# Two head layers' projections in three rounded terms, with the norm's scale and shift folded into weights and biases

## The chip, the cores and the metric

One core of a Trainium2 chip runs the kernel. The metric is the time of one execution on the device, in microseconds (us); a change of a few us in some 2060 is looked for.

## What is computed

The input is x, 16 batches of 256 tokens by 256 features, and a context of the same shape. Four layers follow one another, each added to x:

```python
x = x + L0_xattn(layernorm(x), ctx)          # cross attention, one head
x = x + L0_ffn(x)                            # norm, 32 heads of 8, wo, experts by place, gelu
x = x + L1_xattn(layernorm(x), ctx)          # cross attention with a self score
x = x + L1_ffn(x)                            # norm, 16 heads of 16, wo, norm, router, top 2 of 8 experts

# the part that the change is about, in both ffn layers:
xn = (x - mu) / sqrt(var + 1e-5) * ln_g + ln_b
q, k, v = xn @ wq + bq, xn @ wk + bk, xn @ wv + bv     # no bq, bk, bv in L0
```

All is fp32. The kernel before computes these six projections as fp32 matmuls, the scores of the heads from k and q that are each split into a rounded number and its rest (fp32r, the type in which PE multiplies at the faster rate).

## The kernel before

The batches go through six parts: A (first cross attention), B1 (norm and k, q, v of the 32 heads), B2 (wo, residual, FFN), C (second cross attention), D1 (norm and k, q, v of the 16 heads), D2 (wo, norm, router's logits); HB and HD are the heads themselves. Behind the last batch come the routing and a stage of experts, which has three rounded terms already (line 1837).

The parts of several batches run at once, in 19 rounds r = -1 to 17. Each engine has its own in-order program, cut into steps, and the steps belong to threads: S (scores, line 903, and their maxima, line 1270), T (turn of the maxima), E (exponentials, lines 940 and 1519), V (values, line 955), P (B2, C and D1 of batch r-1, the functions lin2), Q (A and B1 of batch r+1, D2 of batch r-2, the functions lin1), R (routing). A string of letters per round says in which order the threads take their next step, the same on all engines; twelve of the rounds (r = 2 to 13) use the string ORDER. In a round the heads of D1 of one batch and of B1 of the next have their scores; then the round's end holds B1 and D1 of the batches behind them.

At the end of such a round stand, in this order on PE: the turn of NP (line 847; NP is the normed x of D1), B1's key product, a turn of the maxima (MT, line 920), D1's key and query products, B1's query product, D1's and B1's value products, the turn of CXA (the next context), and then the first scores of the heads whose keys and queries D1 has just made. Names that end in Q belong to lin1, in P to lin2.

- `product` (line 854) makes a projection: four fp32 matmuls 128x128x256 (two output halves, two input halves), shown as 8 records.
- `take_cols` (line 1507) on ACT copies the turned norm out of PSUM with the norm's gain as scale and its shift as bias, one instruction for each half, into nTQ or nTP. `take` (line 1500) does so without scale, in one instruction of 128x512.
- The rounded head of the keys and queries is ACT's (line 1591, 1595 for B1, one instruction; line 1645 for D1, two with a bias), its rest is DVE's `rest` (line 1254 for B1, line 1252 for D1). Tiles are used again: qTQ, PRQ, pTQ, cTQ hold B1's keys, rests, queries, rests, and PRP, pTP, cTP, cxTP those of D1; nTQ is the tile of the turned norm.
- SP writes heads and rests to k_dram and q_dram (`put`, line 620, 16 issues in a round) and reads them back in the layout of the scores into KS and QS (`fetch`, line 626). The scores of D1's heads wait for that.
- `norm` on DVE (lines 1231 to 1244) needs POOL's power (line 748) in the middle.
- XF is the sum behind wo in B2 (it is in PRP); its turned copy XFT is in qTP. ACT copies it out of PSUM (line 1500) just ahead of the FFN's first product.

Of the kernel before, what the change touches and what calls it, by code (L numbers as in the profile page):

```python
# [20 lines left out]
F32 = mybir.dt.float32  # L21
# [6 lines left out]
P = 128  # L28
# [94 lines left out]

SECOND = "SPTSEQEQSPQEETEVVSSSQTSSTSPQSSEQPSQPSEEPTSPESQPVPESEVVPSPETPPPSPESQQPEPVSEVQSEQTSQEQQVSPPEQSPEPPVETQEVEQPPEVPPPEPQV"
# [7 lines left out]
def schedule(n, threads):  # L132

    def round_(r, par, b=True, p=True, a=True, d=True, order=ORDER):  # L140
        running = threads(r, par, b, p, a, d)
        for name in order:
            next(running[name])

    round_(-1, 1, b=False, p=False, d=False)
    round_(0, 0, p=False, d=False, order=SECOND)
    round_(1, 1, d=False, order=THIRD)
    for r in range(2, n - 2):
        round_(r, r % 2)
    round_(n - 2, 0, order=FOURTH)  # L150
    round_(n - 1, 1, a=False, order=EARLY)
    round_(n, 0, b=False, a=False, order=LATE)
    round_(n + 1, 1, b=False, p=False, a=False, order=LAST)
# [232 lines left out]
def layers(nc, a, out, scratch, sem, ident, ones, cst, logits, bank, routes):  # L386
# [13 lines left out]
    with ExitStack() as stack:  # L400
# [3 lines left out]
        def tile(name, dt=F32):  # L404
            return sb(name, [P, 2, D], dt)


        MA, WA, MC, WvC = tile("MA"), tile("WA"), tile("MC"), tile("WvC")
        wB = {n: tile(f"wB_{n}") for n in ("wq", "wk", "wv", "wo")}
        wD = {n: tile(f"wD_{n}") for n in ("wq", "wk", "wv", "wo")}  # L410
        wr = sb("wr", [P, DC, NE])
        cols, b1T = sb("cols", [P, 24]), sb("b1T", [P, B, FC])
# [6 lines left out]
        X0, CXA, XBA, NQ, nTQ, cxTQ, qTQ, PRQ, pTQ, cTQ = (  # L419
            tile(n) for n in ("X0", "CXA", "XBA", "NQ", "nTQ", "cxTQ", "qTQ", "PRQ", "pTQ", "cTQ"))  # L420
        X1, Y = [tile(f"X1{i}") for i in range(2)], [tile(f"Y{i}") for i in range(2)]
        zTQ, KHQ, KLQ, QHQ, QLQ = nTQ, qTQ, PRQ, pTQ, cTQ
# [4 lines left out]
        AOP, X2, XBP, NP, nTP, CXC, cxTP, qTP, PRP, pTP, cTP, YB = (  # L427
            tile(n) for n in ("AOP", "X2", "XBP", "NP", "nTP", "CXC", "cxTP", "qTP", "PRP", "pTP", "cTP", "YB"))
        X3 = [tile(f"X3{i}") for i in range(2)]
        AOTP, XF, XFT, prT, YD, zTP = nTP, PRP, qTP, pTP, X2, nTP  # L430
# [10 lines left out]
        HT = sb("HT", [P, FC, 2 * P])  # L441
# [56 lines left out]
        def col(name, c):  # L498
# [8 lines left out]
        s_spare, s_fill = sem("s_spare"), sem("s_fill")  # L507
        SPARES, FILLS = (8, 16), 4
# [12 lines left out]
               "B1": Events(sem("dve_B1"), "bn mv uw n kl ql"), "HB": Events(sem("dve_HB"), "rh0 os0 rh1 os1 rh2 os2 rh3 os3"),  # L521
               "B2": Events(sem("dve_B2"), "xf x"),
               "C": Events(sem("dve_C"), "bn mv uw n c0 c max mxs mxc nb z rs diag x"),
               "D1": Events(sem("dve_D1"), "bn mv uw n kl ql v"), "HD": Events(sem("dve_HD"), "rh0 os0 rh1 os1"),
# [312 lines left out]
        def _(t):  # L837
# [19 lines left out]

            t.transpose(bank[0][:, 0:NV], vecs, ident[0:NV, 0:NV])
# [101 lines left out]

            def threads(r, par, b_, p_, a_, d_):
                hd, hb = lined_up(r, b_, d_)
                last = hd[1] if hd else hb[1] if hb else None
                shared = {}
                if last:
                    h, b = last
                    shared = {"os": (h.os, now(t, b * h.groups + h.groups)), "shifted": (h.shifted, now(t, b * h.twos + h.twos))}
# [24 lines left out]
            def lin1(b, e, par, a_, d_):  # L992
# [8 lines left out]
                if a_:  # L1001
                    wait(t, act, "A", b, "cxT")
                    wait(t, dve, "A", b, "n")
                    turn(5, NQ).then_inc(*E.tick("nT"))
                yield
                if a_:
                    wait(t, act, "A", b, "nT")
                    product(5, MA, nTQ).then_inc(*E.tick("qT"))
                yield
                if a_:  # L1010
                    wait(t, act, "A", b, "qT")
                    product(5, qTQ, cxTQ).then_inc(*E.tick("s"))
                yield
                if a_:
                    wait(t, act, "A", b, "exp")
                    turn(5, PRQ).then_inc(*E.tick("pT"))
                yield
# [1013 lines left out]
```

## Time and profile before

| what | value |
|---|---|
| median of 3 runs | 2061.82 us (2059.59 to 2388.49) |
| profiled execution, its own time | 2058.43 us |
| its span in the trace | 2056.6 us |
| busy share of PE, DVE, ACT, POOL | 92%, 66%, 48%, 29% |
| mean granted clock of PE | 0.952 |

A row of the timeline gives the start, the length, the engine, the line, what is written from what, the shape and in brackets the idle time ahead of it with what ended it. "x8" means that eight records of a kind follow each other; the length then runs from the first one's start to the last one's end. A granted clock of 1.00 is 2.4 GHz, one of 0.50 is 1.2 GHz. The busy share of a whole span mixes stretches with different limits, so what a step is worth is read in its own stretch.

### The profile page before, as it was taken

Reading aid. Unit: us, or ns where it says so; the run is one execution under the profiler, and the core shown is the slowest. Engines: PE = TensorE matmul, PEld = TensorE weight load, DVE = VectorE, ACT = ScalarE, POOL = GpSimd, SP = SyncE. Lnnn points to the kernel's source line nnn. Section 1 sums busy time; section 2 is a strip of 40 time slices with the busy share of each in tenths; the row PEclk is TensorE's granted clock in tenths of the full one; section 3 lists DMA queues with packets and bytes.
Section 4 is the critical chain, followed back from the end, with each engine's and each line's share of the span. In section 5 each row is a group of like instructions: output and inputs, shape, how many; then the busy total and the mean of one; then the engine's idle time right before and its main releaser. Section 6 shows DMA issues by size and latency. Waiting matters only on the chain. (4 is left out here: it accounts for less than half of the span.)

```text
span 2056.6 us, 37550 instructions
## 1 busy us (share of the span) xinstructions
PE 1890.6 (92%) x13657; PEld 1445.2 (70%) x13657; DVE 1353.9 (66%) x3466; ACT 994.1 (48%) x1956; POOL 606.2 (29%) x490
## 2 busy tenths in 40 slices
PE   5699999999999999999999999999887659999998
PEld 4466767777766767677776777766666439999997
DVE  2456667676767767675766767676765457677664
ACT  1255556565556556555655656655343223333332
POOL 0102131221303121220313121230223046777674
PEclk8789999999999999999999999999989759999999
DMA  5223441515244351514344251414120254444231
GB/s 191 87 88 124 139 159 65 175 55 170 100 131 145 122 175 50 174 65 159 122 151 152 73 175 55 165 60 149 59 78 11 72 178 91 119 91 88 43 44 25
DMA packets 205704, 224.86 MB, mean 109 GB/s; under 512 B 15083, under 2 KB 195248, under 8 KB 205520
## 3 DMA queue, kind: packets, MB, share of 16 engines
q1 hardware_dynamic: 191136, 206.40, 30.3%
q0 software_dynamic: 14384, 16.06, 4.8%
q8 instruction: 109, 1.79, 0.4%
q14 instruction: 75, 0.61, 0.1%
HBM read 150.82 MB, written 72.52 MB: 109 GB/s over the span
## 5 line engine op out<-in xcount | busy, mean ns | idle before, releaser
L1270 DVE TENSOR_REDUCE MX<-bank 128x2 f32<-128x512 f32 x768 | 493.1, 683 | 200.4 <-PE bank L903 199.4
L1519 ACT ACTIVATE PT<-bank 128x512 f32<-128x512 f32 x768 | 417.6, 598 | 228.9 <-PE bank L940 227.6
L903 PE MATMUL bank<-KS,QS 32*128 32x256 f32 (+1 forms) x1536 | 194.6, 332 | 45.2 <-DMA QS<-q_dram 26.0
L955 PE MATMUL bank<-PT,VA 128*32 128x256 f32 x3072 | 214.1, 398 | 5.4 <-ACT PT L1519 2.3
L903 PEld LDWEIGHTS bank<-KS,QS 32*128 32x128 f32 (+1 forms) x1536 | 120.5, 193 | 124.9 <-DVE MX L1270 44.4
L940 PE MATMUL bank<-QM,KS 32*128 32x256 f32 (+1 forms) x1536 | 194.5, 332 | 9.8 <-ACT PT L1519 8.7
L1872 ACT ACTIVATE hid<-bank,b1T 128x512 f32<-128x512 f32 x128 | 87.8, 686 | 227.8 <-PE bank L1824 227.8
L748 POOL TENSOR_TENSOR rrC<-uwC,cst 128x4 f32<-128x4 f32 x16 | 16.3, 1019 | 583.1 <-DVE uwC L1239 583.1
L940 PEld LDWEIGHTS bank<-QM,KS 32*128 32x128 f32 (+1 forms) x1536 | 119.0, 190 | 95.7 <-ACT PT L1519 45.5
L1837 PE MATMUL bank<-W2h,hTh 128*128 128x256 f32 x512 | 142.7, 279 | 0.0
L1837 PE MATMUL bank<-W2l,hTh 128*128 128x256 f32 x512 | 141.4, 276 | 0.0
L1837 PE MATMUL bank<-W2h,hTl 128*128 128x256 f32 x512 | 141.3, 276 | 0.0
L955 PEld LDWEIGHTS bank<-PT,VA 128*32 128x32 f32 x3072 | 83.5, 111 | 74.4 <-issue 22.8
L1776 POOL DMA_INDIRECT out_dram<-yo,put x64 | 108.8, 1700 | 81.4 <-DVE yo L1962 68.1
L854 PE MATMUL bank<-qTP,W 128*128 128x256 f32 x512 | 123.8, 389 | 0.0
L1295 DVE TENSOR_TENSOR QM<-QS,bank 128x512 fp32r<-128x512 f32 x128 | 87.3, 682 | 54.5 <-PE bank L920 54.0
L1119 PE MATMUL bank<-W,HT 128*128 128x256 f32 x512 | 122.8, 388 | 0.0
L748 POOL TENSOR_TENSOR rrD<-uwD,cst 128x4 f32<-128x4 f32 x32 | 32.6, 1018 | 280.0 <-DVE uwD L1239 280.0
L1119 PEld LDWEIGHTS bank<-W,HT 128*128 128x128 f32 x512 | 93.6, 190 | 17.4 <-ACT HT L1618 0.4
L854 PEld LDWEIGHTS bank<-qTP,W 128*128 128x128 f32 x512 | 93.2, 190 | 17.6 <-issue 0.4
L1531 ACT ACTIVATE OS<-bank 128x256 f32<-128x256 f32 x192 | 74.6, 388 | 51.5 <-PE bank L955 50.8
L1837 PEld LDWEIGHTS bank<-W2l,hTh 128*128 128x128 f32 x512 | 96.2, 188 | 0.0
(331 smaller groups left out, 3865.4 us busy)
## 6 DMA issues: line engine op xcount, KB each, us to landing
W<-in_L_ffn_w_dram SPq DMA_DIRECT2D x48, 1024.0 KB, 7.4
KS<-k_dram SPq DMA_DIRECT2D x64, 512.0 KB, 6.9
QS<-q_dram SPq DMA_DIRECT2D x64, 512.0 KB, 8.3
k_dram<-qTQ SPq DMA_DIRECT2D x32, 256.0 KB, 2.5
q_dram<-pTQ SPq DMA_DIRECT2D x32, 256.0 KB, 2.7
k_dram<-PRP SPq DMA_DIRECT2D x32, 256.0 KB, 2.5
q_dram<-cTP SPq DMA_DIRECT2D x32, 256.0 KB, 2.8
X<-in_x_dram SPq DMA_DIRECT2D x16, 256.0 KB, 7.0
```

Of the source, the lines that this page charges most:

```text
L854: i = mm(halves(b)[:, o, :], lhsT[:, c, o * P:(o + 1) * P], rhs[:, c, :], start=c == 0, stop=last and c == 1)
L903: x = mm(halves(u)[:, r, :], Q[strip, slot, r * P:(r + 1) * P], K[strip, slot, :], start=True, stop=True)
L940: x = mm(halves(2 + u)[:, kc, :], K[strip, slot, kc * P:(kc + 1) * P], QM[strip, slot // 2 % 2, slot % 2, :], start=True, stop=True)
L955: x = mm(bank[4][SLOT * j:SLOT * (j + 1), 0:D], V[:, kc, n * per:n * per + SLOT], PT[:, n % 8, kc, :], start=kc == 0, stop=kc == 1, tile_p ...
L1119: x = mm(halves(7)[:, r, :], HT[:, f, r * P:(r + 1) * P], W2[:, f, :], start=f == 0, stop=f == FC - 1)
L1270: v.tensor_reduce(MX[:, slot % 4, j, :], halves(u), AX, ALU.max, negate=True).then_inc(h.maxed, 1)
L1295: v.tensor_tensor(QM[:, two % 2, :, :], QS[h.width][:, 2 * two:2 * two + 2, :].bitcast(F32), bank[4][:, D:2 * D].unsqueeze(1).broadcast_to ...
L1519: s_.activation(PT[:, n % 8, :, :], halves(2 + n % 2), ACT.Exp, scale=h.scale).then_inc(h.exp, 1)
L1531: s_.activation(OS[h.width][:, grp, :], bank[4][:, 0:D], ACT.Copy).then_inc(h.os, 1)
L1776: g.indirect_dma_start(out=out, out_offset=bass.IndirectOffsetOnAxis(ap=put[:, n:n + 1], axis=0), in_=yo[u % 2][:, r, :], in_offset=None, ...
L1837: x = mm(bank[YB[r]][:, 0:D], hT[p][:, f, r * P:(r + 1) * P], W2S[i][q][:, f, :], start=(n, f) == (0, 0), stop=(n, f) == (len(TERMS) - 1, ...
L1872: s_.activation(hid[:, f % 4, :], bank[HB[f % 4]][:, :], ACT.Relu, bias=b1T[:, e, f:f + 1]).then_inc(s_hid, 1)
```

## The change

The projections of B1 and D1 no longer take the normed x with gain and shift. Gain is multiplied into the weights once (w g = wh + wl, wh rounded by ACT, wl by DVE), the shift goes into six vectors and a row (K_B, Q_B, K_D, Q_D added to keys and queries, Y_B behind wo of B2, a row for D1's values). In every batch the turned norm is split into zh (ACT, rounded) and zl (DVE, the rest), and a product is wh zh + wl zh + wh zl, twelve fp32r matmuls instead of four fp32 ones. Tiles are laid together for the room: PRP, pTP, cTP and NP become slices of HT (FFN's hidden tile), wl lies over w, zh and zl over nTQ, cxTQ, nTP and qTP. D1's keys go to bank 7 and its queries to bank 6. The strings of steps are the same; the threads of all rounds are now chained, so that one generator runs on through the rounds. Core of the diff:

```diff
-    def round_(r, par, b=True, p=True, a=True, d=True, order=ORDER):
-        running = threads(r, par, b, p, a, d)
+    parts = [threads(*each) for each in rounds]
+    running = {name: chain(*(part[name] for part in parts)) for name in parts[0]}
+    for order in (FIRST, SECOND, THIRD, *[ORDER] * (n - 4), FOURTH, EARLY, LATE, LAST):
         for name in order:
             next(running[name])
...
+        low_names = [f"{x}_{n}" for x in ("wlB", "wlD") for n in QKV] + ["zhQ", "zlQ", "zhP", "zlP"]
...
+        HT = sb("HT", [P, FC, 2 * P])
+        PRP, pTP, cTP, NP = (HT[:, 2 * i:2 * i + 2, :] for i in range(4))
...
+            def by_weights(b, w, zh, zl, part, rnd, same=False):
+                hi, lo = w
+                if same:
+                    wait(t, dve, part, rnd, "zl")
+                for o in range(2):
+                    cut = slice(o * P, (o + 1) * P)
+                    for c in range(2):
+                        mm(halves(b)[:, o, :], hi[:, c, cut], zh[:, c, :], start=c == 0, stop=False)
+                        mm(halves(b)[:, o, :], lo[:, c, cut], zh[:, c, :], start=False, stop=False)
+                    if o == 0 and not same:
+                        wait(t, dve, part, rnd, "zl")
+                    for c in range(2):
+                        i = mm(halves(b)[:, o, :], hi[:, c, cut], zl[:, c, :], start=False, stop=c == 1)
+                return i
...
+            def folded(at, w, vec, bk=4):
+                for o in range(2):
+                    for c in range(2):
+                        i = mm(bank[bk][:, at + o:at + o + 1], w[:, c, o * P:(o + 1) * P], vec(c), start=c == 0, stop=c == 1)
+                return i
...
                     wait(t, act, "B1", b, "zT")
-                    product(5, wB["wk"], zTQ).then_inc(*E.tick("k"))
+                    by_weights(5, (whB["wk"], wlB["wk"]), zhQ, zlQ, "B1", b, True).then_inc(*E.tick("k"))
...
                 wait(t, act, "D1", b, "zT")
-                product(6, wD["wk"], zTP).then_inc(*E.tick("k"))
+                by_weights(7, (whD["wk"], wlD["wk"]), zhP, zlP, "D1", b).then_inc(*E.tick("k"))
...
+            def low(part, b, bnk, head, dst):
+                wait(v, act, part, b, "zT")
+                v.tensor_tensor(dst[:, :, :], halves(bnk), head[:, :, :].bitcast(F32), ALU.subtract).then_inc(*dve[part].tick("zl"))
+            def lows(weights, heads, lows_, gain, high, done):
+                for k, n in enumerate(("wk", "wq", "wv")):
+                    v.wait_ge(high, k + 1)
                     for c in range(2):
+                        x = v.scalar_tensor_tensor(lows_[n][:, c, :], weights[n][:, c, :], col(gain, c), heads[n][:, c, :].bitcast(F32), ALU.mult, ALU.subtract)
+                    x.then_inc(done, 1)
...
                 if a_:
+                    for c in range(2):
+                        x = s_.activation(KHQ[:, c, :].bitcast(F32R), halves(5)[:, c, :], ACT.Identity, bias=fold[:, K_B + c:K_B + c + 1])
+                    x.then_inc(*act["B1"].tick("kh"))
...
+                    if first(b):
+                        for n in ("wk", "wq", "wv"):
+                            heads(wD[n], whD[n], "L1_ffn_ln1_g", s_whD)
...
-                take("B2", 6, XFT, b, "xfT")
+                take_cols("B2", 6, XFT, b, "xfT", "xfT", bias=lambda c: fold[:, Y_B + c:Y_B + c + 1])
```

DVE at the end of one of the twelve rounds, before (NP is D1's normed x, PRQ and cTQ the rests of B1's keys and queries, pTP and cxTP those of D1, MX and MT the maxima):

```order
L1244 TENSOR_SCALAR NP<-X,mvD,rrD 128x256 x2
L1270 TENSOR_REDUCE MX<-bank 128x2 x2
L1278 CAST MT<-MX 128x4x2 x2
L1282 TENSOR_TENSOR MT<-MX,MT 128x4x2 x2
L1254 TENSOR_TENSOR PRQ<-bank,qTQ 128x512
L1295 TENSOR_TENSOR QM<-QS,bank 128x512
L1252 SCALAR_TENSOR_TENSOR pTP<-bank,cols,PRP 128x256 x2
L1252 SCALAR_TENSOR_TENSOR cxTP<-bank,cols,cTP 128x256 x2
L1254 TENSOR_TENSOR cTQ<-bank,pTQ 128x512
```

The same place after (HT is now NP, then D1's key tiles; zlQ and zlP are the rests of the turned norms of B1 and D1):

```order
L1300 TENSOR_SCALAR HT<-X,mvD,rrD 128x256 x2
L1313 TENSOR_TENSOR zlQ<-bank,zhQ 128x512
L1336 TENSOR_REDUCE MX<-bank 128x2 x2
L1344 CAST MT<-MX 128x4x2 x2
L1348 TENSOR_TENSOR MT<-MX,MT 128x4x2 x2
L1313 TENSOR_TENSOR zlP<-bank,zhP 128x512
L1307 SCALAR_TENSOR_TENSOR PRQ<-bank,fold,qTQ 128x256 x2
L1361 TENSOR_TENSOR QM<-QS,bank 128x512
L1307 SCALAR_TENSOR_TENSOR HT<-bank,fold,HT 128x256 x2
L1307 SCALAR_TENSOR_TENSOR cxTP<-bank,fold,HT 128x256 x2
L1307 SCALAR_TENSOR_TENSOR cTQ<-bank,fold,pTQ 128x256 x2
```

Two subtractions of 128x512 came in, one behind D1's norm ahead of the maxima and one behind the turn of the maxima; the rests of B1's keys and queries are two instructions each instead of one.

DVE in the first round, around batch 1's first norm (bnA, mvA, uwA, NQ), before:

```order
L1254 TENSOR_TENSOR PRQ<-bank,qTQ 128x512
L1254 TENSOR_TENSOR cTQ<-bank,pTQ 128x512
L1231 BN_STATS bnA<-X 128x6 x2
L1235 BN_AGGR mvA<-bnA 128x2 x2
L1238 TENSOR_SCALAR uwA<-mvA 128x2
L1239 TENSOR_SCALAR uwA<-mvA 128x2
L1244 TENSOR_SCALAR NQ<-X,mvA,rrA 128x256 x2
```

And after (whD and wlD are the rounded weights of D1 and their rests):

```order
L1313 TENSOR_TENSOR zlQ<-bank,zhQ 128x512
L1307 SCALAR_TENSOR_TENSOR PRQ<-bank,fold,qTQ 128x256 x2
L1307 SCALAR_TENSOR_TENSOR cTQ<-bank,fold,pTQ 128x256 x2
L1487 TENSOR_TENSOR rowbvD<-bank,rowbvD 128x256
L1320 SCALAR_TENSOR_TENSOR wlD_wk<-wD_wk,cols,whD_wk 128x256 x2
L1320 SCALAR_TENSOR_TENSOR wlD_wq<-wD_wq,cols,whD_wq 128x256 x2
L1320 SCALAR_TENSOR_TENSOR wlD_wv<-wD_wv,cols,whD_wv 128x256 x2
L1287 BN_STATS bnA<-X 128x6 x2
L1291 BN_AGGR mvA<-bnA 128x2 x2
```

An addition and the six subtractions of D1's weights now stand between the rest of batch 0's queries (cTQ) and batch 1's first norm.

ACT at the same place before (VA are B1's values, cxTQ the turned context of batch 1):

```order
L1507 ACTIVATE nTQ<-bank,cols 128x256 x2
L1591 ACTIVATE qTQ<-bank 128x512
L1595 ACTIVATE pTQ<-bank 128x512
L1602 ACTIVATE VA<-bank 128x32x8 x2
L1500 ACTIVATE cxTQ<-bank 128x512
```

And after:

```order
L1600 ACTIVATE zhQ<-bank 128x512
L1697 ACTIVATE qTQ<-bank,fold 128x256 x2
L1703 ACTIVATE pTQ<-bank,fold 128x256 x2
L1711 ACTIVATE VA<-bank 128x32x8 x2
L1605 ACTIVATE whD_wk<-wD_wk,cols 128x256 x2
L1605 ACTIVATE whD_wq<-wD_wq,cols 128x256 x2
L1605 ACTIVATE whD_wv<-wD_wv,cols 128x256 x2
L1587 ACTIVATE cxTQ<-bank 128x512
```

ACT's six roundings of D1's weights stand between VA and cxTQ; the turned norm is one instruction instead of two, and B1's keys and queries are two instead of one.

## Rows read from the trace of the kernel before

**Rows 1.** The page's head and part 1 (busy us, share, instructions):

```profile
span 2056.6 us, 37550 instructions
...
PE 1890.6 (92%) x13657; PEld 1445.2 (70%) x13657; DVE 1353.9 (66%) x3466; ACT 994.1 (48%) x1956; POOL 606.2 (29%) x490
```

**Rows 2.** Windows: us, busy us per engine, granted clock, DMA share, GB/s:

```profile
573.90:577.30 3.40, 0.60 (x5) 0.46 (x6) 0.00 (x0) 0.60 (x1) 0.00 (x0) 1.00 1.09 357
577.40:580.70 3.30, 3.30 (x17) 2.74 (x16) 2.24 (x7) 0.60 (x1) 0.00 (x0) 0.50 1.09 348
576.70:650.20 73.50, 72.31 (x563) 53.52 (x563) 56.48 (x150) 43.10 (x88) 13.07 (x12) 0.98 0.25 80
759.61:831.73 72.12, 70.85 (x563) 52.22 (x563) 56.35 (x150) 43.10 (x88) 13.07 (x12) 1.00 0.27 89
```

**Rows 3.** Timeline of PE, 829.9 to 852 (start, length, x records, idle before):

```profile
831.73 0.66 PE L847 MATMUL bank<-cst,NP 128*128 128x128 f32 x4 [1.06 <-DVE NP L1244]
832.22 1.89 PE L854 MATMUL bank<-nTQ,wB_wk 128*128 128x256 f32 x8
833.95 0.38 PE L920 MATMUL bank<-cst,MT 128*128 128x128 f32 x2
...
851.19 0.50 PE L903 MATMUL bank<-KS,QS 64*128 64x256 f32 x4 [2.03 <-DMA QS<-q_dram]
```

**Rows 4.** PE's waits by line and cause (us in total, times, longest):

```profile
PE bank L903 <- DMA QS<-q_dram: 26.0, 15, 5.5
```

**Rows 5.** Timeline of ACT and DVE, 829 to 842:

```profile
829.42 2.25 DVE L1244 TENSOR_SCALAR NP<-X,mvD,rrD 128x256 f32<-128x256 f32 x2
...
832.42 1.02 ACT L1507 ACTIVATE nTP<-bank,cols 128x256 f32<-128x256 f32 x2 [0.74 <-PE bank L847]
...
834.15 0.60 ACT L1591 ACTIVATE qTQ<-bank 128x512 fp32r<-128x512 f32 x1 [0.71 <-PE bank L854]
...
836.10 0.84 ACT L1645 ACTIVATE PRP<-bank,cols 128x256 fp32r<-128x256 f32 x2 [1.35 <-PE bank L854]
...
836.97 0.87 DVE L1252 SCALAR_TENSOR_TENSOR pTP<-bank,cols,PRP 128x256 fp32r<-128x256 f32 x2 [0.91 <-ACT PRP L1645]
```

**Rows 6.** Timeline of SP's issues, 834 to 852:

```profile
834.83 1.50 SPq L620 DMA_DIRECT2D k_dram<-qTQ  x2
...
842.91 1.16 SPq L620 DMA_DIRECT2D q_dram<-cTQ  x2
...
844.70 0.52 SPq L626 DMA_DIRECT2D QS<-q_dram  x1
```

**Rows 7.** Timeline of PE in the experts stage, 13 records in a row:

```profile
1900.75 0.28 PE L1837 MATMUL bank<-W2h,hTh 128*128 128x256 f32 x1
...
1902.11 0.28 PE L1837 MATMUL bank<-W2h,hTh 128*128 128x256 f32 x1
```

**Rows 8.** Groups of DVE by line and form (busy us, mean ns, idle before):

```profile
L1925 DVE TENSOR_TENSOR xgTl<-bank,xgTh 128x512 fp32r<-128x512 f32 x32 | 20.5, 681 | 0.7 <-ACT xgTh L1855 0.7
```

**Rows 9.** Timeline around the turned XF (named qTP), 770.5 to 775:

```profile
772.30 0.59 ACT L1500 ACTIVATE qTP<-bank 128x512 f32<-128x512 f32 x1
...
773.02 2.21 PE L854 MATMUL bank<-qTP,W 128*128 128x256 f32 x9
```

**Rows 10.** Timeline of the first round, 65 to 80:

```profile
66.18 0.74 DVE L1231 BATCH_NORM_STATS2 bnA<-X 128x6 f32<-128x256 f32 x2
...
68.34 0.66 ACT L1602 ACTIVATE VA<-bank 128x256 f32<-128x256 f32 x2 [2.81 <-PE bank L854]
68.76 0.73 DVE L1244 TENSOR_SCALAR NQ<-X,mvA,rrA 128x256 f32<-128x256 f32 x2 [1.21 <-POOL rrA L748]
...
69.82 0.60 ACT L1500 ACTIVATE cxTQ<-bank 128x512 f32<-128x512 f32 x1 [0.81 <-PE bank L847]
...
70.47 0.66 PE L847 MATMUL bank<-cst,NQ 128*128 128x128 f32 x4 [0.75 <-ACT cxTQ L1500]
```

**Rows 11.** Groups of PE by line and form, one-column matmuls:

```profile
L1136 PE MATMUL bank<-ones,pTP 128*128 128x1 f32 x128 | 15.5, 242 | 0.5 <-POOL pTP L817 0.4
```

More of the change, by code:

```diff
@@ L405, in tile @@
             return sb(name, [P, 2, D], dt)
+        QKV = ("wq", "wk", "wv")
+        with ExitStack() as rounded:
+            low_names = [f"{x}_{n}" for x in ("wlB", "wlD") for n in QKV] + ["zhQ", "zlQ", "zhP", "zlP"]
+            lows_at = {n: rounded.enter_context(nc.sbuf_tensor(n, [P, 2, D], F32R)) for n in low_names}
+        wB, wD = ({n: tile(f"{x}_{n}") for n in QKV} for x in ("wB", "wD"))
+        nTQ, cxTQ, nTP, qTP = (tile(n) for n in ("nTQ", "cxTQ", "nTP", "qTP"))
+        wlB, wlD = ({n: lows_at[f"{x}_{n}"] for n in QKV} for x in ("wlB", "wlD"))
+        zhQ, zlQ, zhP, zlP = (lows_at[n] for n in ("zhQ", "zlQ", "zhP", "zlP"))
         MA, WA, MC, WvC = tile("MA"), tile("WA"), tile("MC"), tile("WvC")
-        wB = {n: tile(f"wB_{n}") for n in ("wq", "wk", "wv", "wo")}
-        wD = {n: tile(f"wD_{n}") for n in ("wq", "wk", "wv", "wo")}
+        wB["wo"], wD["wo"] = tile("wB_wo"), tile("wD_wo")
+        whB, whD = ({n: tile(f"{x}_{n}", F32R) for n in QKV} for x in ("whB", "whD"))
         wr = sb("wr", [P, DC, NE])
+        fold = sb("fold", [P, 12])
+        V_B, K_B, Q_B, Y_B, K_D, Q_D = range(0, 12, 2)
         cols, b1T = sb("cols", [P, 24]), sb("b1T", [P, B, FC])
@@ L1008, in lin1 @@
                     product(5, MA, nTQ).then_inc(*E.tick("qT"))
+                    if first(b):
+                        folded(K_B, wB["wk"], lambda c: col("L0_ffn_ln_b", c)).then_inc(s_fold, 1)
                 yield
@@ L1016, in lin1 @@
                     turn(5, PRQ).then_inc(*E.tick("pT"))
+                    if first(b):
+                        folded(Q_D, wD["wq"], lambda c: col("L1_ffn_ln1_b", c)).then_inc(s_fold, 1)
                 yield
@@ L1020, in lin1 @@
                     product(5, CXA, pTQ).then_inc(*E.tick("cT"))
+                    if first(b):
+                        t.wait_ge(s_folded, 1)
+                        folded(Y_B, wB["wo"], lambda c: fold[:, V_B + c:V_B + c + 1]).then_inc(s_fold, 1)
+                        for c in range(2):
+                            i = mm(bank[3][:, 0:D], col("L1_ffn_ln1_b", c).broadcast_to([P, P]), wD["wv"][:, c, :], start=c == 0, stop=c == 1)
+                        i.then_inc(s_fold, 1)
                 yield
@@ L1346, in lin1 @@
                 yield
-                yield from idle(2)
+                if first(b):
+                    v.wait_ge(s_fold, 1)
+                    v.tensor_copy(fold[:, V_B:V_B + 2], bank[1][:, V_B:V_B + 2]).then_inc(s_folded, 1)
+                yield
+                yield
                 if a_:
@@ L1508, in take_cols, with high, heads @@
                 x.then_inc(*act[part].tick(tick))
+            def high(part, bnk, dst, b):
+                wait(s_, pe, part, b, "nT")
+                s_.activation(dst[:, :, :], halves(bnk), ACT.Copy).then_inc(*act[part].tick("zT"))
+            def heads(weight, head, gain, done):
+                for c in range(2):
+                    x = s_.activation(head[:, c, :], weight[:, c, :], ACT.Copy, scale=col(gain, c))
+                x.then_inc(done, 1)
             def exps(h, b, prev):
@@ L1594, in lin1 @@
                     wait(s_, pe, "B1", b, "q")
-                    s_.activation(QHQ[:, :, :].bitcast(F32R), halves(5), ACT.Copy).then_inc(*act["B1"].tick("qh"))
+                    for c in range(2):
+                        x = s_.activation(QHQ[:, c, :].bitcast(F32R), halves(5)[:, c, :], ACT.Identity, bias=fold[:, Q_B + c:Q_B + c + 1])
+                    x.then_inc(*act["B1"].tick("qh"))
                 yield
```

113 lines of the change are left out of this document (71 added, 42 removed).

## The prediction

> **What bounds the kernel now.** I read the page first [rows 1]: PE is busy for 92% of the span, so a change that makes PE's work cheaper looks promising. That share is a mean, so I looked next, with the windows and the timeline, at where the six projections of a steady round stand. A round lasts about 91 us (scores of the next batch at 759.61 and 851.19, [rows 2, 3]) and has two stretches with different limits.
>
> - From the first scores to the turn of NP (759.61 to 831.73) PE is busy for 70.85 of 72.12 us [rows 2]. This stretch is bound by PE, but no key, query or value projection stands in it: all six come behind the turn of NP.
> - From the turn of NP to the next scores (831.73 to 851.19, [rows 3]) PE has work nearly throughout, and then still waits 2.03 us for QS to land. Over the kernel this wait is 26.0 us in 15 stalls [rows 4], about 1.7 each. The chain that ends there starts with the turn of NP and PE's B1 key product (832.22 to 834.11); ACT rounds it (834.15 to 834.75, [rows 5]); SP issues the first put at 834.83 and the following ones (eight pairs) nearly back to back until 844.07, then the fetch of KS, and that of QS at 844.70 [rows 6]. QS is there about 6 us later. The other five products finish while SP still issues: they lie beside the chain.
>
> So a cheaper product shortens what PE does ahead of a wait for a transfer, and the transfer's start hangs on the B1 key product alone.
>
> **The change part by part.**
>
> *The products.* An fp32 product here is 8 records in 832.22 to 833.95, a step of 0.216 and 1.73 us in all [rows 3]. The new product is 12 fp32r matmuls of the same shape. The experts stage has such terms already: 12 steps from 1900.75 to 1902.11, 0.113 each, so 1.36 us [rows 7]. That saves 0.37 us per product; 6 per batch over 16 batches are 96, and 96 x 0.37 = 35.5 us is all that there is to win.
>
> *The turned norm before the products.* Two ACTs of 1.02 together (nTP, [rows 5]) become one of 128x512, 0.60 by qTQ's row; a subtraction of the same size on DVE is added, 0.68 [rows 8]. B1's key product now waits for this low part. DVE does it behind NP's norm (done at 831.67), so about 832.3 instead of 832.22: 0.1 to 0.2 late. The product is 0.37 shorter; the rounding of the keys becomes two ACTs with a bias, 0.84 (PRP's row) instead of 0.60. Sum on the chain: +0.15 − 0.37 + 0.24, about 0. D1's low part stands on DVE behind the turn of the maxima, which itself comes 0.68 later; PE's turn of MT (833.95) then waits some 0.5, and D1's keys are rounded within 0.1 of where they were. SP has its puts queued till then, so nothing there is late. I take +0.15 per round on the chain; the bounds are −0.3 (the low part is hidden) and +0.7 (its whole length adds). The loop has twelve such rounds: 1.8 us.
>
> *PE beside the chain.* 6 x 0.37 = 2.2 us less work, minus the waits just named: the stall before the scores grows by about 1.5, from 2.03 to some 3.5. That alone costs nothing in the stall, but the clock may react. After the longest steady stall, in 573.90 to 577.30 with 0.60 us of PE work, the granted clock was 0.50 (1.2 of 2.4 GHz) from 577.40 to 580.70, and the stretch up to the turn of NP took 73.50 instead of 72.12 us [rows 2]: 1.38 more. Behind the stall of 2.03 us the clock stayed up. With stalls of about 3.5 I take a drop in every second of the twelve rounds, 6 x 1.38 = 8.3 us (bounds 0 and 12 x 1.38 = 16.6). The Trainium skill, TensorE: Matmul & The Clock Gate, section Loop structure matters more than you think, gives a wait for a transfer between bursts of matmuls as the pattern that lets the clock fall. By that rule every round would pay; by the stalls shown here only the longest did.
>
> *XFT.* One ACT of 0.60 becomes two with a bias, 0.84. It stands in the PE-bound stretch: ACT's qTP (this is XFT) ends at 772.89 and PE's product with it starts at 773.02 [rows 9], directly behind the scores, so 0.13 of the 0.24 are hidden by PE's work and the rest, with the queue behind it, is late: 0.1 to 0.24, taken as 0.2. Twelve rounds: 2.4 us.
>
> *The first round.* Here one batch runs alone and the chain from engine to engine sets the time [rows 10]. ACT gets six weight tensors to round, each two ACTs of 0.84 to 1.02; those of D stand between VA (done at 69.00) and cxTQ (69.82). DVE gets one addition of 128x256 and six subtractions of weight rests, two of 0.43 each (pTP's row has 0.87 for two); those of D stand ahead of bnA (66.18). They wait for ACT's rounding: VA at 69.0, three pairs of 0.84 to 1.02 bring 71.5 to 72.1, the last pair on DVE 72.5 to 73.0. bnA then starts at about 73.0 instead of 66.18; from it to the end of NQ's norm are 3.31 us, so NQ comes at 76.3 and its turn on PE near 76.4 instead of 70.47. That is +5.9. B's weights are rounded earlier, while PE and ACT wait for each other. The folded shifts add to PE's queue in batch 0's A part six groups of 8 records with one column (0.242 by the nearest row [rows 11], so at most 1.9 us a group) and one broadcast product, most of which lies in PE's waits for ACT; I take +1.0. B1's three shorter products in this chain give back 1.1, and the low part and the two-part roundings cost part of that: −0.4. Later slack regains some: +5.5 in all (bounds 3 and 8).
>
> *The last rounds.* Batches 14 and 15 have no next batch beside their D1, so PE waits up to 5.5 us for QS [rows 4] with little in between; their products lie on the chain, 2 x 2 x 0.37: −1.3 us (0 to −2.5).
>
> *No cost.* The tiles that now share HT, wB, wD and the nT tiles add waits that are met tens of microseconds before; the order of the steps is unchanged, so no DMA issue moves past another; setup loads are the same.
>
> *Sum*, against the profiled execution of 2058.43 us (span 2056.6): 5.5 + 1.8 + 8.3 + 2.4 − 1.3 = +16.7, so 2075 us. The median of the runs shown, 2061.82, lies 0.2% above that execution, which changes nothing in the sum.
>
> **The rivals.**
>
> 1. *PE's gain arrives.* If the puts and the fetch are not what holds the scores, but PE's own queue ahead of them, then the round shortens by 2.2 and pays only XFT's 0.2: 2058.4 + 5.5 + 2.4 − 35.5 = 2031 us. For it: PE's total share of 92%. Against it: PE idles at nearly every one of these scores, and QS is named [rows 3, 4]. Half of it (the chain gets 0.3 shorter each round, the first round hides its roundings, no drop in the clock) would be near 2050.
> 2. *The clock drops in each round* (the rule of the skill above says so, but its price is this kernel's own): 12 x 1.38 = 16.6 in place of 8.3, so 2083 us; with two such stretches per round, because the chain in the tail is then itself slower, 2100 us. For it: the one stall of 2.9 us was enough. Against it: shorter stalls left the clock alone, and PE still has 14 us of work in the tail.
> 3. *The other side: the three-term products are not cheaper.* If the new terms, each with a fresh weight tile of 128x128, go at fp32's step of 0.216, a product takes 12 x 0.216 = 2.59 instead of 1.73. In a tail that is 6 x 0.86 = 5.2 us more, 2.0 of which the stall absorbs, and the key product's 0.86 is on the chain. About 3.2 each in 12 rounds, some 15 in the four chain-bound batches, and 5.5 for the first round give 2117 us. It decides as soon as a term takes more than 0.144 (1.73/12). Against it: the 0.113 of the experts stage, with the same shapes and a weight load per term.
>
> **How the numbers follow.** The forecast (first round, half the rounds with a drop) has 0.58, with its own range 2062 to 2085. PE's gain in full has 0.08, half of it 0.13; the clock in each round 0.12 near 2083 and 0.06 near 2100; dearer terms 0.03. From 2036 to 2096 everything is held but the full gain, dearer terms and half of the 2100 case, that is a little under 2 in 10. A change of 2% is about what a measurement of this kernel tells from none. Faster by that (below 2020) needs all of PE's gain and a free first round: 0.03. Slower by that (above 2102) needs dearer terms, or two drops a round with a first round at its upper bound: 0.07. Within 2%: 0.90.
>
> **What would show it.** In the profile after: a product of 12 records in about 1.36 us; in a steady tail the first put within 0.3 of 3.1 us behind the turn of NP, as before, and the wait of the scores for QS longer, some 40 us in all instead of 26; the stretch from scores to NP at 72.3 us, and 73.7 where the clock was 0.50 in it; bnA of batch 1 behind the six weight rests and the second batch's first scores about 5 us later. The prediction is wrong if the rounds are 1 us or more shorter than 91.6 (rival 1: then something ahead of the B1 keys got faster), if more than nine or none of the twelve rounds show the half clock, or if the first round's loss is outside 3 to 8 us.

## The result, and the profile after

| | before | after |
|---|---|---|
| median | 2064.03 us (4 runs, 2059.59 to 2388.49) | 2088.61 us (4 runs, 2082.86 to 2100.62) |
| ratio, with its 95% interval | | 1.0134 [1.0075, 1.0193] |
| profiled execution, span | 2058.43, 2056.6 | 2088.91, 2087.1 |
| span up to the first scores of D1's heads | 209.76 | 217.82 |
| the twelve rounds behind them | 1099.69 | 1113.30 |
| the rest | 747.18 | 755.98 |

The changed kernel is slower by 1.3%: the interval lies above 1, and below the 2% that a measurement of this kernel tells from no change. The run of 2388.49 us is a slow one and stands outside the ratio. The last three rows cut the two profiled spans at the first and at the thirteenth of those scores in PE's timeline. The loss between the two profiles has three parts: +8.1, +13.6 and +8.8 us. In 22 runs beside the first experiments the kernel before took 2045.7 to 2071.68 us, so some 10 us between two single executions can be chance; which of the three parts hold is shown below.

The page's head and part 1 for the changed kernel:

```profile
span 2087.1 us, 38566 instructions
...
PE 1895.3 (91%) x14093; PEld 1475.8 (71%) x14093; DVE 1386.5 (66%) x3547; ACT 998.8 (48%) x1984; POOL 603.4 (29%) x490
```

PE is busy for 1895.3 us, as before (1890.6, [rows 1]), though its products got cheaper, so other work of PE must have got dearer. The mean granted clock fell from 0.952 to 0.938.

A drop is a stretch in which the granted clock is 0.50 instead of 1.00. Windows of the changed kernel (us; busy us of PE, PEld, DVE, ACT, POOL; granted clock, DMA share, GB/s): the stretch from the scores to the turn of NP, first in a round without a drop and then in one with it; then, from a third round, the stall ahead of the scores and the drop that begins 0.77 us behind the start of these scores:

```profile
217.82:290.03 72.21, 70.92 (x562) 52.27 (x563) 56.32 (x150) 43.03 (x88) 13.07 (x12) 1.00 0.28 91
...
399.88:473.49 73.61, 72.34 (x563) 53.64 (x563) 56.59 (x150) 43.10 (x88) 13.07 (x12) 0.98 0.27 88
676.87:678.87 2.00, 0.01 (x2) 0.01 (x2) 0.00 (x0) 0.60 (x1) 0.00 (x0) 1.00 1.05 349
679.64:683.05 3.41, 3.41 (x18) 2.86 (x17) 2.47 (x7) 0.60 (x1) 0.00 (x0) 0.50 1.09 350
```

The first row answers to 759.61:831.73 in [rows 2]: 72.21 instead of 72.12 at full clock. Ten of the twelve rounds have a drop there. Seven of them look like the second row, 73.5 to 73.8 at a mean clock of 0.98; the others take 74.1, 75.0 and 75.0, the last two with some 6.5 us at 0.50. The last two rows show what goes ahead of such a drop: 2.00 us without work on PE, then 3.41 us at 0.50. Before, one of twelve rounds had that. That the one brings the other is tested in experiments 1 and 2.

PE's waits in the twelve rounds, from their first scores to the thirteenth, first before, then after (us in total, times, longest):

```profile
PE bank L903 <- DMA QS<-q_dram: 19.7, 13, 2.9
```

```profile
PE bank L943 <- DMA QS<-q_dram: 33.4, 13, 4.4
...
PE bank L960 <- DVE MT L1348: 3.2, 12, 0.3
```

The wait for QS grew from 19.7 to 33.4 us in 13 stalls, from 1.5 to 2.6 each, and a wait for MT came in, 3.2.

The end of a steady round after, on PE (the turn of NP, B1's key product from its first record, the turn of MT, D1's value product from its first to its last record, the scores):

```profile
937.77 0.66 PE L853 MATMUL bank<-cst,HT 128*128 128x128 f32 x4 [1.05 <-DVE HT L1300]
938.46 0.35 PE L872 MATMUL bank<-zhQ,whB_wk 128*128 128x256 f32 x1
...
940.39 0.44 PE L960 MATMUL bank<-cst,MT 128*128 128x128 f32 x2 [0.27 <-DVE MT L1348]
...
945.59 0.28 PE L886 MATMUL bank<-whD_wv,zhP 128*128 128x256 f32 x1
...
946.91 0.28 PE L888 MATMUL bank<-whD_wv,zlP 128*128 128x256 f32 x1
...
956.52 0.80 PE L943 MATMUL bank<-KS,QS 64*128 64x256 f32 x4 [2.35 <-DMA QS<-q_dram]
```

These answer to [rows 3]. The B1 key product starts 0.69 behind the turn (0.49 before). From 945.59 to 946.91 are 11 steps from record to record, so 0.120 each and 1.44 us for a product of 12. SP's first put and the fetch of QS:

```profile
941.08 0.87 SPq L626 DMA_DIRECT2D k_dram<-qTQ  x2
...
951.24 0.48 SPq L632 DMA_DIRECT2D QS<-q_dram  x1
```

The first put comes 3.31 us behind the turn of NP (3.10 before, [rows 6]), and QS is fetched 10.2 us behind it (9.9 before): the chain stayed about as long as it was.

### The profile page after: what moved, and what is told of

Read it like the earlier page. It is cut to its first block and busy times, and to the rows that moved or that the text cites. A ratio compares the mean times of both kernels' runs of the same rounds, so it can differ in the third digit from the quotient of the medians.

```text
span 2087.1 us, 38566 instructions
## 1 busy us (share of the span) xinstructions
PE 1895.3 (91%) x14093; PEld 1475.8 (71%) x14093; DVE 1386.5 (66%) x3547; ACT 998.8 (48%) x1984; POOL 603.4 (29%) x490
## 5 line engine op out<-in xcount | busy, mean ns | idle before, releaser
L995 PE MATMUL bank<-PT,VA 128*32 128x256 f32 x3072 | 213.4, 397 | 5.2 <-ACT PT L1617 2.8
L754 POOL TENSOR_TENSOR rrC<-uwC,cst 128x4 f32<-128x4 f32 x16 | 16.3, 1019 | 611.5 <-DVE uwC L1295 611.5
L860 PEld LDWEIGHTS bank<-qTP,W 128*128 128x128 f32 x512 | 93.3, 190 | 19.7 <-ACT qTP L1594 4.0
```

Source lines behind the costliest of these rows:

```text
L860: i = mm(halves(b)[:, o, :], lhsT[:, c, o * P:(o + 1) * P], rhs[:, c, :], start=c == 0, stop=last and c == 1)
L995: x = mm(bank[4][SLOT * j:SLOT * (j + 1), 0:D], V[:, kc, n * per:n * per + SLOT], PT[:, n % 8, kc, :], start=kc == 0, stop=kc == 1, tile_p ...
```

## The experiments

The stretches named in the text are differences of starts in PE's timeline of the run; "the rounds" are always the twelve.

### 1. More work for PE in the changed kernel

```diff
                     wait(t, dve, "B1", b, "ql")
+                    by_tokens(5, zhQ, zlQ, (whB["wv"], wlB["wv"]))
                     by_tokens(5, zhQ, zlQ, (whB["wv"], wlB["wv"])).then_inc(*E.tick("v"))
```

> The changed kernel with B1's value product made twice in every batch (1.7 us more of PE work just ahead of the wait for QS, the first result overwritten by the same one). Theory (the clock): the loss in the twelve steady rounds is the drop of PE's clock behind the longer stall. The stall shrinks from about 2.7 to about 1.0 us on average, most of the drops go, the stretch from the scores to the turn of NP falls from 73.7 to 72.2 us in at least eight rounds: 10 to 17 us faster than the changed kernel, though it does more. Rival (the added instructions of DVE and ACT lengthen the rounds, the clock only goes along): drops stay or not, the rounds are no shorter; the same time, or up to 12 x 1.7 = 20 us slower where PE sets it.

Measured: 2078.94 us (7 runs, 2074.83 to 2081.37), 1.0088 [1.0056, 1.012] of before. That is 10 us less than the changed kernel, with 16 products more, but the two intervals overlap, and experiment 11 has the changed kernel at 2075.65; the total alone shows no gain. The rounds do. All twelve, then the stretch behind the scores in a round without a drop and in the only one that has a drop there, and the wait for QS:

```profile
216.91:1318.39 1101.48, 1069.72 (x8641) 802.73 (x8641) 792.99 (x2112) 645.54 (x1333) 242.85 (x204) 0.99 0.38 125
307.55:379.83 72.28, 70.93 (x562) 52.19 (x563) 56.35 (x150) 43.23 (x89) 13.07 (x12) 1.00 0.27 91
677.09:750.65 73.56, 72.28 (x562) 53.56 (x562) 56.55 (x150) 43.13 (x88) 13.09 (x12) 0.98 0.25 83
```

```profile
PE bank L943 <- DMA QS<-q_dram: 13.8, 12, 2.4
```

The rounds take 1101.5 us instead of 1113.3. The wait for QS fell from 33.4 to 13.8 us and the drops behind the scores from ten to one. The stretches from the scores to the turn of NP sum to 869.2 us; in the changed kernel they took 884.1, before 867.1. So 14.9 of the 17.0 us that this stretch had lost came back, by PE doing more. The ends of the rounds (turn of NP to the next scores) took 3.1 us of that again: four of them now have half clock, as three had before (see the last section). In this stretch the clock is the cause of the loss, not something that goes along with it. What is left, 72.28 against 72.12, is looked for in experiment 7.

### 2. Less work for PE in the kernel before

The query and value products of B1 and D1 sum half of their inputs; the rest of the sum is left out.

```diff
+            def half_product(b, lhsT, rhs):
+                for o in range(2):
+                    i = mm(halves(b)[:, o, :], lhsT[:, 0, o * P:(o + 1) * P], rhs[:, 0, :], start=True, stop=True)
+                return i
...
-                    product(5, wB["wq"], zTQ).then_inc(*E.tick("q"))
+                    half_product(5, wB["wq"], zTQ).then_inc(*E.tick("q"))
```

> The kernel before; B1's and D1's query and value products sum only half of their inputs (two of four matmuls left out each), nothing else is touched: 4 x 0.87 = 3.5 us less of PE work in each round's tail. Theory (the clock): the stall ahead of the scores grows to 3 us and more, the clock drops in nearly each of the twelve rounds, each loses about 1.4 us: 10 to 17 us slower than before, less 3 to 5 us that the rounds without a neighbour gain. Rival (the added instructions): the same time as before in the steady rounds, 3 to 5 us faster in all.

Measured: 2061.31 us (10 runs, 2058.29 to 2064.63), 1.0011 [0.9985, 1.0036]. A stall ahead of the scores, the half clock behind it, and the stretch from these scores to the turn of NP:

```profile
845.47:849.76 4.29, 0.00 (x2) 0.01 (x2) 0.00 (x0) 0.60 (x1) 0.63 (x1) 1.00 0.93 304
850.54:853.90 3.36, 3.36 (x18) 2.81 (x17) 2.44 (x7) 0.60 (x1) 0.00 (x0) 0.50 1.09 349
849.76:923.23 73.47, 72.28 (x563) 53.51 (x563) 56.46 (x150) 43.09 (x88) 13.05 (x12) 0.98 0.28 91
```

The drops came, in eleven of twelve rounds, with nothing of the change in the kernel: the stretches to the turn of NP sum to 883.3 us, 16.2 more than before. The total missed the expectation of 10 to 17 us slower. The ends of the rounds got 0.9 us shorter on average (18.5 instead of 19.4), 10.6 in all, which I had not counted, and the start and the end of the kernel 2 to 3 us each. Four half products, 3.5 us of PE work per round, are taken away, and the kernel is no faster.

### 3 and 4. The scores behind three turns

```diff
-ORDER = "QQSPPQSPPQTSPQ...
+ORDER = "QQPPQSSPPQTSPQ...
```

> The changed kernel; in the string of the twelve rounds the first scores step is moved behind the two turns of OS and the turn of NQ, on all engines (QQPPQS for QQSPPQ): 2.5 us of useful PE work stand where PE waited for QS. Theory: the stall falls from 2.7 to under 1 us, the clock stays up, each round is 2 to 3 us shorter by the stall and 1.4 by the clock: 35 to 50 us faster than the changed kernel, some 2043 us. Rival: the maxima of the moved scores come later, so PE waits at the turn of the maxima instead; within 10 us of the changed kernel.

> The kernel before with the same move of the first scores step. Theory: its stalls of 1.0 to 2.9 us are filled, so 12 x 1.4 = 17 us and one drop of the clock go: about 2043 us; the changed kernel with the same move is then 5 us faster to 5 us slower than this one, since there the whole of its cheaper products is had, less the start. Rival: PE waits for the maxima instead, same as before, 2060.

Measured: 2089.15 us (4 runs; 1.0136 [1.0084, 1.0188]) for the changed kernel and 2067.2 (10 runs; 1.0036 [1.0006, 1.0065]) for the one before. The rival held. PE's waits in the rounds of the changed kernel with the move (its profiled execution was the slowest of the four, 2099.36 us):

```profile
PE bank L943 <- DVE MX L1336: 17.5, 13, 1.4
PE bank L943 <- DMA QS<-q_dram: 15.6, 12, 3.2
```

The wait for QS is halved, 33.4 to 15.6, but the next scores follow at once and wait for DVE's maxima, 17.5 us where there were 0.2; in the kernel before with the move that wait is 17.9. In the changed kernel the half clock stayed: each round but the first needs 73.5 us or more from its scores to the turn of NP, though 2.5 us of that stretch's work now stand ahead of it.

### 5 and 6. B1's queries behind the fetch

```diff
                 if a_:
                     ...
                     put(8, "k", True)
                 yield
+                yield
                 if a_:
                     made(act, "B1", b, "qh")
                     put(8, "q", False)
                     made(dve, "B1", b, "ql")
                     put(8, "q", True)
-                yield
-                if a_:
                     for c in range(DC):
                         ...
                         fetch(8, b, c)
```

> The changed kernel; on SP the four puts of B1's queries and their rests are issued behind the fetch of D1's keys and queries instead of ahead of it. Theory (SP's queue behind the B1 keys is what holds the scores): the fetch is issued about 2 us earlier, the stall ahead of the scores falls from 2.7 to about 0.7 us, each of the twelve rounds is 2 us shorter, and with the drops of the clock gone 1.4 more: 25 to 42 us faster than the changed kernel, about 2052. Rival (the DMA engines' bandwidth holds the transfer, not its issue): QS lands no earlier, same time as the changed kernel.

> The kernel before with the same move on SP. Theory: its stalls (1.5 us on average) go, 12 x 1.5 = 18 us faster, about 2042; then the rounds are bound by PE, and the changed kernel with the move should be up to 12 x 0.5 us shorter in these rounds and lose its start. Rival: same time as before.

Measured: 2060.78 us (10 runs, 2048.89 to 2071.92; 1.0024 [1.0003, 1.0045]) for the changed kernel, 28 less than without the move; 2047.09 (10 runs, 2037.86 to 2054.56; 0.9941 [0.9916, 0.9967]) for the kernel before, 12 less than the 2059.07 measured beside it. The profile of the changed kernel here is of the fastest of its ten executions (2048.89 us), so its rounds show the move at its best. SP's issues at the end of a round of the changed kernel with the move:

```profile
1099.43 1.73 SPq L626 DMA_DIRECT2D k_dram<-qTQ  x2
...
1108.22 0.37 SPq L632 DMA_DIRECT2D QS<-q_dram  x1
...
1109.79 1.52 SPq L626 DMA_DIRECT2D q_dram<-pTQ  x2
```

The fetch of QS is issued 8.8 us behind the first put instead of 10.2, and B1's queries (pTQ, cTQ) behind it. The scores follow 5.0 us behind that issue, 5.3 without the move: the transfer takes about as long as it did, it only starts earlier. So SP's queue was what held the scores. The rounds, and one end of a round, first of the changed kernel, then of the one before:

```profile
210.00:1295.98 1085.98, 1050.37 (x8497) 782.37 (x8497) 793.59 (x2112) 644.37 (x1333) 242.49 (x204) 0.99 0.39 127
...
1096.11:1113.22 17.11, 15.82 (x148) 12.37 (x148) 9.74 (x27) 10.59 (x23) 7.13 (x6) 1.00 0.73 232
```

```profile
553.64:571.00 17.36, 17.02 (x124) 12.30 (x124) 8.27 (x23) 9.95 (x21) 7.05 (x6) 1.00 0.77 248
211.35:1295.46 1084.11, 1065.04 (x8209) 780.29 (x8209) 775.82 (x2064) 644.69 (x1320) 241.79 (x204) 0.99 0.39 127
```

The rounds come to 1086.0 and 1084.1 us; their ends alone are 18 and 15 us shorter than without the move, the rest of the changed kernel's gain is mostly drops that went. In the kernel before PE is busy for 17.02 of 17.36 us at the end of a round: PE sets it now. In the changed kernel it is busy for 15.82 of 17.11: the cheaper products are there, 1.2 us of PE time, and the chain over SP still takes 17.1. This is where the gain goes: with the queue as it was, PE already waited 1.5 us per round before and 2.6 after.

### 7. XFT in one instruction

The folded shift Y_B is left out of XFT.

```diff
-                take_cols("B2", 6, XFT, b, "xfT", "xfT", bias=lambda c: fold[:, Y_B + c:Y_B + c + 1])
+                take("B2", 6, XFT, b, "xfT")
```

> The changed kernel with XFT copied by one ACT instruction again (it leaves out the folded shift Y_B behind wo). By my step: the stretch from the scores to the turn of NP, at full clock, is 0.1 to 0.2 us shorter (72.24 to 72.11), 2 us in all. Rival: the 0.15 us come from DVE or PE elsewhere in the round, and the stretch stays at 72.24.

Measured in one execution: a stretch from the scores to the turn of NP without a drop, and one with it:

```profile
214.03:286.08 72.05, 70.84 (x562) 52.20 (x562) 56.35 (x150) 42.80 (x88) 13.07 (x12) 1.00 0.28 93
305.07:378.59 73.52, 72.33 (x563) 53.54 (x563) 56.59 (x150) 42.86 (x87) 13.08 (x12) 0.98 0.28 90
```

72.05 instead of 72.21 in the first of the twelve rounds, which took 72.05 in the kernel before too, and 73.5 instead of 73.6: the second instruction costs 0.16 us per round, 1.9 in all. The execution took 2080.34 us, but single executions lie 10 us apart for other reasons, so only the stretch counts here.

### 8. D1's weights a batch later

```diff
-                    if first(b):
+                    if isinstance(b, int) and b == 1:
                         for n in ("wk", "wq", "wv"):
                             heads(wD[n], whD[n], "L1_ffn_ln1_g", s_whD)
```

The rests on DVE are moved in the same way. First the rows of the changed kernel: the first of ACT's roundings, DVE's last rest, bnA and the turn of NQ, and two of the one-column groups of batch 0:

```profile
72.44 0.91 ACT L1605 ACTIVATE whD_wk<-wD_wk,cols 128x256 fp32r<-128x256 f32 x2
...
74.97 0.88 DVE L1320 SCALAR_TENSOR_TENSOR wlD_wv<-wD_wv,cols,whD_wv 128x256 fp32r<-128x256 f32 x2
...
75.77 0.75 DVE L1287 BATCH_NORM_STATS2 bnA<-X 128x6 f32<-128x256 f32 x2
...
79.24 1.09 PE L853 MATMUL bank<-cst,NQ 128*128 128x128 f32 x4 [5.96 <-DVE NQ L1300]
```

```profile
39.02 1.71 PE L895 MATMUL bank<-cols,wB_wk 128*128 128x1 f32 x8
...
46.89 0.95 PE L895 MATMUL bank<-cols,wD_wq 128*128 128x1 f32 x8
```

> The changed kernel; ACT's six roundings of D1's weights and DVE's six rests are made behind batch 1's B1 part instead of batch 0's. Theory: batch 1's first norm and the turn of NQ come about 6 us earlier (70.5 to 73.5 us instead of 79.2), and the first scores of D1's heads (217.8) 5 to 6 us earlier; 5 to 6 us faster than the changed kernel in the whole. Rival: the next wait of the first round (the second batch's B1) takes most of it back, 0 to 2 us.

Measured: 2089.33 us (4 runs, 2085.96 to 2090.55; 1.0152 [1.0106, 1.0198]). DVE's bnA, then PE's turn of NQ:

```profile
70.00 0.74 DVE L1287 BATCH_NORM_STATS2 bnA<-X 128x6 f32<-128x256 f32 x2
```

```profile
73.66 0.66 PE L853 MATMUL bank<-cst,NQ 128*128 128x128 f32 x4 [0.75 <-ACT cxTQ L1588]
```

bnA starts at 70.00 instead of 75.77 and the turn at 73.66 instead of 79.24, as expected, but the first scores of D1's heads come at 218.63 (217.82 without the move). The rival held. The moved rests now stand ahead of the next batch's norm, and PE waits for that one:

```profile
135.76 0.88 DVE L1320 SCALAR_TENSOR_TENSOR wlD_wv<-wD_wv,cols,whD_wv 128x256 fp32r<-128x256 f32 x2
136.56 0.74 DVE L1287 BATCH_NORM_STATS2 bnA<-X 128x6 f32<-128x256 f32 x2
140.02 1.06 PE L853 MATMUL bank<-cst,NQ 128*128 128x128 f32 x4 [4.91 <-DVE NQ L1300]
```

Without the move this bnA starts at 136.67 and this turn at 141.33. Batch 1's B1 key product was still some 6 us ahead; here 1.3 us are left, and by the first scores of D1's heads nothing.

### 9 and 10. All of B1's puts behind the fetch

The key puts are moved behind the fetch too (the same edit as in 5, with both blocks).

> The changed kernel; on SP all eight puts of B1 (keys and queries) are issued behind the fetch of D1's. Theory: with the B1 puts out of the way the chain is the turn of NP, D1's products, their roundings, eight puts and the fetch, about 1.2 us shorter than with B1's queries alone moved; the changed kernel's round is bound by PE only at 72.25 + some 15.7 us, so it gains: the stretch from the turn of NP to the scores falls from a median of 17.4 (queries alone moved) to about 16.3, twelve rounds from 1086 to about 1074 us, 10 us faster than with the queries alone, about 2050 in the median. Rival (the bandwidth of the transfers, or the maxima, hold the round by now): the same as with the queries alone moved.

> The kernel before with the same move. Theory: PE itself sets its rounds since the move of the queries (stall -0.07 in seven of twelve), so nothing more comes: 2047 us, twelve rounds at 1084. Then the difference to the changed kernel with this move is what the cheaper products are worth in the steady rounds, about 10 us of the 12 x 2.2 that they save on PE.

Measured: 2099.26 us (4 runs; 1.0223 [1.0195, 1.0251]) and 2065.93 (6 runs; 1.0045 [1.0008, 1.0082]). Both expectations fell, for a reason that neither side had. The end of the round did shrink, to 16.3 to 17.5 us in eight of the twelve in the changed kernel, but the stretch behind the scores, 72.2 us at full clock without any move, took between 73.8 and 78.6. ACT's next use of the tile qTQ, which holds B1's rounded keys till they are written, and PE's wait behind it:

```profile
967.86 0.84 ACT L1592 ACTIVATE qTQ<-bank,qkbias 128x256 f32<-128x256 f32 x2 [4.47 <-DMA q_dram<-cTQ]
```

```profile
PE bank L858 <- ACT qTQ L1592: 25.7, 11, 3.5
```

ACT waits 4.47 us till the last of the late puts, that of cTQ, has landed, and PE loses 25.7 us in eleven waits. In the kernel before with this move PE loses 17.0 us in the same place, and with the queries alone moved the changed kernel has four such waits already, 3.4 us. So the move says nothing on what the cheaper products are worth; that stays where experiments 5 and 6 left it.

### 11. The changed kernel again

> The changed kernel as it is, once more, for a second profile. Theory: again a drop of the clock in ten to twelve of the twelve steady rounds, 1113 us for them within 3; the part ahead of the first scores of D1's heads 210 to 220 us. If the drops were chance in the first profile, there are about one to four.

Measured: 2075.65 us in one execution. The rounds:

```profile
211.78:1324.94 1113.16, 1058.92 (x8497) 791.35 (x8497) 795.46 (x2112) 644.17 (x1332) 242.54 (x204) 0.98 0.38 124
```

1113.16 against 1113.30 us: the loss in the rounds, with eleven drops, comes again to a tenth of a us. The other two parts do not: the first scores of D1's heads stand at 211.78 (217.82), the rest takes 748.9 us (755.98).

## Why the prediction was right, and where it was off

The forecast was 2075, with 0.90 on a change of less than 2%; measured were 2088.6, or 1.3%. That is outside the range of the main case (2062 to 2085) and nearest to the second rival (the clock drops in each round, 2083). Two of the prediction's own signs of being wrong came true: more than nine of the twelve rounds have the half clock, and the first round's loss lies outside 3 to 8 us. So the direction of the loss and its place in the rounds were right, and the size of the clock's part was not. By its steps:

- *What bounds the kernel.* Right. No product stands in the stretch bound by PE, and the chain over B1's keys and SP's queue sets the end of the round. The first put came 3.31 us behind the turn of NP, within the 0.3 of 3.1 that was named. Experiments 5 and 6 show the queue as the bound: with four puts out of it the ends of the rounds of the two kernels are shorter by 18 and 15 us in all.
- *The products.* 1.44 us instead of 1.36: the step is 0.120 here, 0.113 in the experts stage. A product saves 0.29, not 0.37, so the most that was to be had was about 28 us. The third rival (0.216 a step) is out.
- *The clock: the term that was mis-sized.* I took a drop in every second round, 8.3 us; there were ten of twelve in one profile and eleven in the other. The stretch up to the turn of NP lost 17.0 us, 1.9 of it by XFT, so the clock cost 15.1. Experiments 1 and 2 show both directions: with work put in the drops go, with work taken out of the kernel before they come. The mechanism is the second rival's, at its price of 1.38 us in seven of the ten drops (1.3 to 1.6 us above 72.2); in three the half clock lasted longer and cost 1.9 to 2.8. What I had of it was wrong in one detail: the stalls did not grow to 3.5 us but from 1.5 to 2.6 on average (19.7 and 33.4 us over 13), partly because PE waits for MT as well, and already that was enough. The Trainium skill, TensorE: Matmul & The Clock Gate, section Loop structure matters more than you think, has a near pattern: a "long DMA wait between every matmul", behind which PE "goes cold". Here one such wait stands in a round of some 92 us, and the trace after agrees in ten of twelve rounds; before, with stalls of 1.5 us on average, it agreed in one.
- *The chain, +1.8.* The first put came 0.2 us later than in most rounds before, but the ends of the rounds sum to 229.2 us instead of 232.6. The three ends with half clock in the kernel before (20.6, 19.3 and 20.9) make that difference: the other nine take 19.1 on average, as the twelve do after. So nothing is shown of +0.15 or of a gain.
- *XFT, +2.4.* Right, 1.9 by experiment 7 (0.16 per round).
- *The sum of the rounds.* 1.8 + 8.3 + 2.4 = 12.5 us were forecast and 13.6 and 13.5 measured. That they lie so near is luck: the clock behind the scores cost 6.8 us more than forecast, and the ends gave 3.4 back where 1.8 were to be paid.
- *The first round, +5.5.* The mechanism is as written: bnA stands behind the last of the rests of D1's weights. How much it costs is read from batch 0's turn of NQ (in B1) to batch 1's (70.47 before, [rows 10], and 79.24 after). Batch 0's turn before and after, then both turns in the second profile of the changed kernel:

```profile
55.49 1.12 PE L847 MATMUL bank<-cst,NQ 128*128 128x128 f32 x4 [4.32 <-DVE NQ L1244]
```

```profile
59.21 1.12 PE L853 MATMUL bank<-cst,NQ 128*128 128x128 f32 x4 [4.32 <-DVE NQ L1300]
```

```profile
54.85 1.12 PE L853 MATMUL bank<-cst,NQ 128*128 128x128 f32 x4 [4.32 <-DVE NQ L1300]
74.87 1.09 PE L853 MATMUL bank<-cst,NQ 128*128 128x128 f32 x4 [5.50 <-DVE NQ L1300]
```

  That is 20.03 us after (79.24 − 59.21), 20.02 in the second profile, 14.98 before and 14.83 in experiment 8: the weights cost 5.1 us at this place, 5.9 were forecast. The other 3.7 of the shift at 79.24 stand ahead of batch 0's turn, and the second profile does not have them: from 30 to 45 us the mean granted clock was 0.51 in the first profile after, 0.84 in the second and 0.73 before, and at half clock a group of folded shifts takes 1.71 us in front of PE's next product. Why the clock differs there is open. By the first scores of D1's heads the two profiles stand at +8.06 and +2.02, both outside the 3 to 8 that were named. Over all eight profiles with the change and its variants these scores come at 215.1 on average, over the five without it at 209.7: +5.4, with single ones at 210.0 to 220.6 and 206.9 to 213.4.
- *The last rounds, −1.3.* No gain is shown: +8.8 and +1.8. This is the largest miss of the first profile, 10 of the 13.8 us between its loss (30.5) and the forecast (16.7). About half of the difference between the two profiles lies in one round, from the scores of batch 13 to those of batch 14, whose rows in the first and in the second profile of the changed kernel are:

```profile
1427.89:1547.31 119.42, 104.28 (x756) 77.59 (x756) 84.27 (x218) 47.93 (x96) 28.43 (x22) 0.87 0.26 85
```

```profile
1421.69:1537.71 116.02, 100.85 (x757) 75.78 (x758) 84.84 (x220) 47.81 (x96) 28.42 (x22) 0.91 0.25 83
```

119.4 us at a mean clock of 0.87 and 116.0 at 0.91; before, it took 114.4 at 0.91. The products that were to give 1.3 us back stand in a stretch whose clock decides more. Whether the change makes it lower there or chance did is open: the rest takes 748.9 to 762.8 us in the eight profiles with the change and 745.1 to 759.4 in the five without.
- *The sum.* The second profile lost 17.2 us in all, within 0.5 of the forecast, but as 2.0, 13.5 and 1.8 where 5.5, 12.5 and −1.3 were forecast. That agreement is luck; the 13.5 is the part that comes again.

## What to carry to other kernels

Before a product is made cheaper, find the transfer that PE waits for behind it, and follow that transfer back through the queue that issues it; here the queue of puts ahead of a fetch hid all that the cheaper products could give, and moving four of them was worth more (12 us in the kernel before) than the change, whose cheaper products brought nothing even then. If the wait stays, less work ahead of it makes it longer, and the clock may then be lost on the work behind it, as in these rounds: a kernel can get slower by the work that it saves. When puts are moved behind something, look who writes their source tile next.

## What the runs showed of the hardware that I had not expected

- Filling a wait with useless matmuls made the twelve rounds 12 us shorter (1101.5 instead of 1113.3 us, experiment 1).
- Stalls of 1.9 to 2.8 us went either way. In the changed kernel there was a drop with a stall of 1.95 us (its scores of 491.85) and none behind 2.51 (308.96); in the kernel before there was none behind 2.28 (943.02), and experiment 2 had none behind its first stall of 2.83. So the length of the stall alone does not decide. Three drops in a row start at 399.74, 491.90 and 584.06 us in the changed kernel, 92.16 apart, while its rounds with a drop last 92 to 94 us. Why one stall counts and another doesn't is not settled by these runs.
- The clock also fell behind a stretch in which PE's records leave hardly a gap, at the end of three of the twelve rounds before, and of four in experiment 1. Windows of the kernel before, ahead of such a drop and behind it:

```profile
457.88:461.29 3.41, 3.31 (x36) 2.50 (x36) 2.96 (x9) 2.72 (x7) 2.64 (x3) 1.00 0.00 0
461.30:464.70 3.40, 3.33 (x25) 2.18 (x18) 3.38 (x5) 2.55 (x6) 3.40 (x4) 0.50 0.27 101
```

PE is busy for 3.31 of 3.41 us, in 36 short records (scores and values of the heads, the router's logits, a turn), and then runs at 0.50. Of the twelve rounds before, the three with such a drop took 20.6, 19.3 and 20.9 us for their end, the others 18.4 to 20.3.
